# A flamingo-style gated block with routed experts: shared tiles scattered twice instead of joined by a product, and full tiles run with their gathered rows as stationary operand

## What is computed

```
# stage 1: sparse attention-like mixing of rows
sim   = mean over 4 heads of Q K^T / sqrt(32), Q = ctx Wq^T, K = ctx Wk^T
thr   = the 153rd largest value of each row of sim
A     = sigmoid(sim) where sim >= thr, else 0;  A = (A + A^T) / 2
x     = x + tanh(g_xattn) * ((1 - gamma) * layernorm(x) + gamma * A)
# stage 2: gated mixture of 8 experts, top 2 per token, plus a shared expert
n     = layernorm(x), 2048 rows
logits = n router_w; the two largest e1, e2 get the weights sigmoid(logit)
shared = silu(n sh_gate) * (n sh_up) sh_down
expert e of a token: xin = prob * n;  h = silu(xin gate_e) * (xin up_e);  y = h down_e
out   = x + tanh(g_ffn) * (shared + sum over the two experts)
```

## Time and profile before

| what | value |
|---|---|
| median of the runs | 395.9 us (395.59, 395.9, 397.62) |
| the profiled execution's own time | 397.11 us |
| its span | 395.4 us |
| TensorE busy | 367.4 us, 93% |
| VectorE busy | 256.2 us, 65% |
| ScalarE busy | 212.1 us, 54% |
| POOL busy (issue of its DMAs and small operations) | 142.1 us, 36% |
| mean granted TensorE clock | 0.978 |
| chain that ended last | TensorE 71%, ScalarE 8%, DMA 7%, DVE 7% |

### The profile page before, as it was taken

One profiled execution on the slowest core, in us unless ns is written; L12 is line 12 of the kernel. 1 busy time (PEld: TensorE's weight loads), 2 busy tenths in 40 slices (PEclk: granted clock), 3 DMA queues, 4 the chain that ended last, 5 costly groups with the idle time before them and its releaser, 6 DMA issues.

```text
span 395.4 us, 7266 instructions
## 1 busy us (share of the span) xinstructions
PE 367.4 (93%) x2372; PEld 233.0 (59%) x2374; DVE 256.2 (65%) x858; ACT 212.1 (54%) x406; POOL 142.1 (36%) x114
## 2 busy tenths in 40 slices
PE   8957889989999999999999999999999999999970
PEld 4313478557845588457875475757545644567750
DVE  1799999999999689960846793645547654623310
ACT  3595788476653686435220575554556565652320
POOL 2200220030533342222215265463656655644422
PEclk9986999999999999999999999999999999999996
DMA  7999971166657633449241755544535353644244
GB/s 218 383 388 382 389 242 37 27 195 182 189 108 170 200 64 34 72 112 206 35 53 35 128 79 90 103 77 85 87 78 91 72 86 76 107 61 87 44 55 53
DMA packets 29357, 51.18 MB, mean 129 GB/s; under 512 B 4614, under 2 KB 7942, under 8 KB 29318
## 3 DMA queue, kind: packets, MB, share of 16 engines
q0 software_dynamic: 9920, 22.16, 34.1%
q1 hardware_dynamic: 19110, 28.40, 20.8%
q10 hardware_dynamic: 288, 0.13, 0.1%
HBM read 28.60 MB, written 22.09 MB: 128 GB/s over the span
## 4 chain that ended last, share of the span: by engine, by line
PE 71%; ACT 8%; DMA 7%; DVE 7%; issue 3%; POOL 1%; SPq 1%; POOLq 1%; DVEq 0%; ACTq 0%
PE gate_up L1317 25%; PE down L1367 15%; PE gate_up L1326 8%; PE gate_up L1332 6%; PE down L1358 4%; PE turned_x L1295 4%; DMA out_dram<-y_sb,idx 3%; ACT junk L713 3%; PE front L1274 2%; DMA xs<-in_x_dram 2%; DMA out_dram<-y_sb,tmp 1%; DMA out_dram<-tmp,idx 1%; PE front L1182 1%; ACT x L750 1%; ACT sim L708 1%
## 5 line engine op out<-in xcount | busy, mean ns | idle before, releaser
L1317 PEld LDWEIGHTS gate_up<-xT,w_shgu 128*128 128x128 f32 x1024 | 117.6, 192 | 11.7 <-issue 10.4
L1317 PE MATMUL gate_up<-xT,w_shgu 128*128 128x128 f32 x1024 | 121.0, 276 | 1.5 <-ACT xT L761 1.1
L565 POOL DMA_INDIRECT xg<-x_rows,idx x34 | 52.2, 1534 | 43.5 <-DMA x_rows<-payl 13.5
L589 POOL DMA_INDIRECT out_dram<-y_sb,idx x20 | 35.9, 1793 | 54.0 <-DMA out_dram<-y_sb,idx 20.9
L815 ACT ACTIVATE y_sb<-down,gates 128x512 f32<-128x512 f32 x42 | 28.8, 687 | 36.5 <-PE down L1367 24.9
L1367 PE MATMUL down<-w_dn,hT 128*128 x100 | 47.0, 596 | 0.0
L2045 DVE COPY sim<-w_gu 128x2048 f32 x36 | 42.1, 1221 | 1.9 <-issue 1.0
L713 ACT ACTIVATE junk<-sim,probe 128x512 int8<-128x512 f32 x44 | 31.2, 712 | 16.8 <-DVE probe L1730 9.9
L2053 DVE COPY w_shgu<-w_gu 128x2048 f32 x16 | 20.0, 1249 | 26.6 <-PE gate_up L1317 17.7
L826 ACT COPY xs<-w_dn 128x1024 f32 x36 | 36.0, 1045 | 2.0 <-issue 1.7
L2074 DVE SCALAR_TENSOR_TENSOR h<-gate_up,p_t,silu 128x256 f32<-128x256 f32 x18 | 8.7, 482 | 42.9 <-ACT silu L784 33.9
(11 more groups left out here) (241 smaller groups left out, 535.0 us busy)
## 6 DMA issues: line engine op xcount, KB each, us to landing
w_gu<-in_L_ffn_gate_up_w_dram SPq DMA_DIRECT2D x8, 1024.0 KB
xs<-in_x_dram SPq DMA_DIRECT2D x4, 1024.0 KB, 7.7
w_dn<-in_L_ffn_down_w_dram SPq DMA_DIRECT2D x8, 512.0 KB
out_dram<-xs SPq DMA_DIRECT2D x4, 1024.0 KB, 6.0
x_rows<-x SPq DMA_DIRECT2D x4, 1024.0 KB, 4.7
out_dram<-y_sb POOLq DMA_DIRECT2D x16, 256.0 KB
w_gu<-in_ctx_dram SPq DMA_DIRECT2D x4, 256.0 KB, 5.8
xg<-x_rows,idx POOLq DMA_INDIRECT x34
```

Source lines behind the costliest of these rows:

```text
L565: G.indirect_dma_start(out=xg[:, t % XG, :], out_offset=None, in_=x2_rows[0:2 * N, :] if t < EARLY else x2_rows[:, :], in_offset=bass.Indi ...
L589: G.indirect_dma_start(out=out[0:2 * N, :] if t < EARLY else out[:, :], out_offset=bass.IndirectOffsetOnAxis(ap=rows, axis=0), in_=y_at(j) ...
L1317: mm = TE.matmul(g_b[j % 2][:, f * P:(f + 1) * P], w_shgu[:, c, f * P:(f + 1) * P], xT[:, x_slot(j), c], start=(c == 0), stop=(c == DC - 1))
```

## The change

- `fold`, `folded_y` and `fold_m` are gone. `find_twins` makes only the marks, and `scatter_rows` makes a second index column `idx_d`: the token's row for the second row of a pair, the spare row for all others. A new POOL helper `scatter_doubles(t)` sends the same output buffer a second time with `idx_d`, for the nine mixed tiles. It is placed behind `scatter(t + 1)` and waits for `scatter(t)` to have landed. The next mixed tile's scatter, the scatter of tile 32 and `y_of` of the buffer's next user wait for it.
- `STAGED`, `stage_full`, the weighing of rows (L2065) and `full_staged` are gone. All 16 full tiles from 10 on stream their weights, and all are turned by `turn_h`.
- The mixed tiles are 9, 11, 13, 15, 18, 21, 24, 27, 30 instead of 9, 12, 15, 18, 20, 22, 24, 26, 28, and the staging copies are moved with them.
- The joining product of tiles 32 and 33 stays.

```diff
-    MIXED = (9, 12, 15, 18, 20, 22, 24, 26, 28)
+    MIXED = (9, 11, 13, 15, 18, 21, 24, 27, 30)
...
             def scatter(t):
...
                 if t == PAIR:
                     rows = idx_p
+                    pool.wait_ge(doubles_out, 16 * MIX)
                     pool.wait_ge(scatter_ready, 1)
                 if m is not None:
-                    pool.wait_ge(folded, m + 1)
+                    if m:
+                        pool.wait_ge(doubles_out, 16 * m)
                     pool.wait_ge(scatter_ready, 1)
...
+            def scatter_doubles(t):
+                m = MIXED.index(t)
+                pool.wait_ge(scattered, 16 * CHAIN.index(t) + 16)
+                G.indirect_dma_start(out=out[:, :], out_offset=bass.IndirectOffsetOnAxis(ap=idx_d[:, m:m + 1], axis=0),
+                                     in_=y_at(job_of("M", t)), in_offset=None, compute_op=ALU.add
+                                     ).then_inc(doubles_out, 16)
...
             def y_of(j):
...
                 if k is not None and is_m(k):
                     act.wait_ge(scattered, 16 * CHAIN.index(JOBS[k][1]) + 16)
+                    if mixed_at(k) is not None:
+                        act.wait_ge(doubles_out, 16 * mixed_at(k) + 16)
...
-            def folded_y(j):
-                act.wait_ge(fold_ps, mixed_at(j) + 1)
-                A.copy(y_at(j), f_b[0][:, :]).then_inc(folded, 1)
...
-            def fold(j):
...
-                TE.matmul(f_b[0][:, :], fold_m[:, m * P:(m + 1) * P], y_at(j), start=True,
-                          stop=True).then_inc(fold_ps, 1)
...
-                if kind == "S" or staged(j):
+                if kind == "S":
                     for f in range(F2 // P):
...
             def find_twins(k):
...
-                    V.tensor_scalar(fold_m[:, m * P:(m + 1) * P], others, row_f[:, m:m + 1], None, ALU.is_equal)
                     ins = V.scalar_tensor_tensor(tmp_flat[:, m * P:(m + 1) * P], others, row_f[:, m:m + 1], upper[:, :],
                                                  ALU.is_equal, ALU.mult, accum_out=twin[:, m:m + 1])
...
                 V.tensor_tensor(idx_s, row_f, unused[:, 0:MIX], ALU.subtract)
+                V.tensor_scalar(idx_d, unused[:, 0:MIX], dump, None, ALU.add)
...
-            def stage_full(t):
...
-                V.tensor_copy(w_shgu[:, :, :].rearrange("p c f -> p (c f)"),
-                              w_gu[:, bass.ds(e * (DC * F2), DC * F2)]).then_inc(full_staged, 1)
...
-                if t in STAGED:
-                    dve.wait_ge(p_ready, t + 1)
-                    V.tensor_scalar(xg[:, r, 0:D], xg[:, r, 0:D], p_t[:, r:r + 1], None, ALU.mult).then_inc(rows_weighed, 1)
```

More of the change, by code:

```diff
@@ L95, in is_m, with m_count @@
         return JOBS[j][0] == "M"
-    STAGED = [t for t in range(EARLY + 1, MT) if t not in MIXED]
-    def staged(j):
-        return JOBS[j][0] == "M" and JOBS[j][1] in STAGED
-    def turned(j):
-        return is_m(j) and not staged(j)
-    def turned_count(j):
-        return sum(1 for k in range(j) if turned(k))
+    def m_count(j):
+        return sum(1 for kind, _ in JOBS[:j] if kind == "M")
     def x_slot(j):
@@ L1020, in _ @@
             y_of(26)
+            turned_h(27)
             stage_down(1, 2)
@@ L1029, in _ @@
             y_of(28)
-            stage_down(2, 0)
-            stage_down(2, 1)
-            folded_y(28)
+            turned_h(29)
+            stage_down(2, 2)
+            stage_down(2, 3)
             silu_of(30)
@@ L1035, in _ @@
             y_of(29)
-            stage_down(2, 2)
-            stage_down(2, 3)
+            turned_h(30)
+            stage_down(3, 0)
+            stage_down(3, 1)
             silu_of(31)
@@ L1044, in _ @@
             y_of(31)
-            stage_down(3, 0)
-            stage_down(3, 1)
-            folded_y(31)
+            turned_h(32)
+            stage_down(4, 0)
+            stage_down(4, 1)
             silu_of(33)
@@ L1050, in _ @@
             y_of(32)
-            stage_down(3, 2)
-            stage_down(3, 3)
+            turned_h(33)
+            stage_down(4, 2)
+            stage_down(4, 3)
             silu_of(34)
@@ L1059, in _ @@
             y_of(34)
-            stage_down(4, 0)
-            stage_down(4, 1)
-            folded_y(34)
+            turned_h(35)
+            stage_down(5, 0)
+            stage_down(5, 1)
             silu_of(36)
@@ L1083, in _ @@
             y_of(38)
-            stage_down(6, 0)
-            stage_down(6, 1)
-            folded_y(38)
+            turned_h(39)
+            stage_down(6, 2)
+            stage_down(6, 3)
             silu_of(40)
@@ L1119, in _ @@
             y_of(44)
-            folded_y(44)
+            turned_h(45)
+            stage_down(8, 2)
+            stage_down(8, 3)
             silu_of(46)
@@ L1123, in _ @@
             y_of(45)
+            turned_h(46)
             silu_of(47)
@@ L1126, in _ @@
             y_of(46)
+            turned_h(47)
             silu_of(48)
@@ L1129, in _ @@
             y_of(47)
+            turned_h(48)
             silu_of(49)
             y_of(48)
+            turned_h(49)
             y_of(49)
@@ L1321, in up @@
                     for c in range(DC):
-                        if c == DC // 2 and folds is not None:
-                            fold(folds)
                         for r in range(4):
@@ L2317, in _ @@
             stage_up(4, 3)
-            gate(35)
-            stage_full(21)
-            weight_of(21)
-            gate(36)
-            weight_of(22)
+            weight_of(17)
+            gate(32)
+            weight_of(18)
+            gate(33)
+            weight_of(19)
+            gate(34)
             stage_up(5, 0)
@@ L2326, in _ @@
             stage_up(5, 3)
+            weight_of(20)
+            gate(35)
+            weight_of(21)
+            gate(36)
+            weight_of(22)
             gate(37)
-            stage_full(23)
-            weight_of(23)
-            gate(38)
-            weight_of(24)
             stage_up(6, 0)
@@ L2335, in _ @@
             stage_up(6, 3)
+            weight_of(23)
+            gate(38)
+            weight_of(24)
             gate(39)
-            stage_full(25)
             weight_of(25)
             gate(40)
-            weight_of(26)
             stage_up(7, 0)
@@ L2344, in _ @@
             stage_up(7, 3)
+            weight_of(26)
             gate(41)
-            stage_full(27)
             weight_of(27)
@@ L2349, in _ @@
             weight_of(28)
+            gate(43)
             stage_up(8, 0)
@@ L2353, in _ @@
             stage_up(8, 3)
-            gate(43)
-            stage_full(29)
             weight_of(29)
```

166 lines of the change are left out of this document (77 added, 89 removed).

## The result

The changed kernel takes 400.4 us (median of six runs, 399.25 to 401.96), the kernel before beside it 395.9. The ratio is 1.010, with a 95% interval of 1.007 to 1.013: **slower by 1.0%**. The profiled execution took 400.57 us with a span of 398.8, against 397.11 and 395.4. The head of its page: engines' busy time with their shares, and the granted clock in 40 slices.

What follows compares the result with a forecast made beforehand. TensorE and the chain of scatters were taken as limits, with the chain deciding. TensorE would end 1.3 us earlier, the chain gain 1.5 (disturbed) to 3.7 (free); taking 1.5 from the median 395.9 gave 394.4 us, range 390.5 to 402.

Steps and rivals of the forecast that it cites:

- POOL becomes the bound: Rival: three issues on POOL between a mixed tile's scatter and the next take triples over 18.0 us; 400.7 us, chance 0.28.
- TensorE, 7.3 us less and 6 given back: On TensorE: folds, ups and weight copies save, turning costs, 7.3 us less; stalls return 3, 0.9 and 2.1; ends 1.3 earlier.
- the stall at job 27: Near 248 us, tile 11's y waits for tile 9's second scatter to free their shared buffer; TensorE stalls 3 us.
- the wait at the end: The last down waits for its turned h, which stands behind the y of job 48 on ScalarE: 2.1 us more.
- The 0.9 us for the gate: The gate of job 26 stands behind four staging copies ending near 234.5 us: 0.9 us given back on TensorE.
- The chain decides: The chain of scatters, at 5.6 us a cycle and 7.6 where doubles are awaited, sets the end rather than TensorE.
- The alternating stretch, tiles 8 to 15: Tile 10's scatter stays at 244.51; each later pair takes 5.6 + 7.6 us, 13.2 on the chain against TensorE's 12.1.
- The triples, 17.9 us: From tile 15, three tiles with one second scatter take 16.8 us plus about 1.1 for lengthened issues, level with TensorE's 18.0.
- the 18.5 that I had named as a sign of being wrong: Sign against the forecast: groups of three tiles with one second scatter taking over 18.5 us.
- Doubles land 3.5 us after their issue: A second scatter's data lands 3.5 us after its issue, bounds 3.3 and 5.5; 6.9 after the preceding scatter's start.
- The tail, 9.5 us: Tile 31's scatter goes at 375.5, tile 32 waits 7.6 us for doubles, tile 33 follows 1.85 behind, at 385.0.
- Issues held for a whole run of copies: Rival: POOL issues wait for all four staging copies, 2.3 us per mixed tile instead of 1.1; 405 us, chance 0.05.

Runs made afterwards that it cites:

- experiment 10: The changed kernel with its gate_up staging copies on VectorE cut to 64 of 2048 columns (mixed tiles use wrong weights): 392.11 us, ratio 0.9904.
- experiment 2: The changed kernel with sixteen filler products on TensorE ahead of the down of job 28: 400.42 us, ratio 1.0109.
- experiments 3 and 7: The changed kernel without its nine second scatters and their waits, 388.19 us; the changed kernel with a bounds check skipping the second scatters' spare rows, 392.59 us.
- experiment 1: The changed kernel with three output buffers from job 24 instead of 26, so job 27 shares none with tile 9: 398.33 us, ratio 1.0044.
- experiment 5: The changed kernel with each of the 36 staging copies of 2048 columns cut into four of 512: 403.56 us, ratio 1.0162.
- experiment 11: The kernel before with its gate_up staging copies cut to 64 of 2048 columns, whole-expert copies kept (mixed tiles use wrong weights): 396.52 us, ratio 1.0004.
- experiment 4: The kernel before with all full tiles streaming their weights and turned, folds and positions of mixed tiles kept: 397.23 us, ratio 1.0019.

## Why the prediction was wrong

I forecast 394.4 us, faster; it is 400.4, slower. My wide range held it, and the rival "POOL becomes the bound" had its time, 400.7. By the steps of the prediction:

- **TensorE, 7.3 us less and 6 given back:** right in its parts. Folds are gone; an up of a full tile adds 3.44 to the chain of waits in experiment 10 and shows as 3.60 in the timeline, where I took 3.49; the stall at job 27 is 3.51 (I took 3), the wait at the end 1.72 (2.1). The 0.9 us for the gate hardly came: the four copies ended at 233.22, where I had 234.5, and the turning of that h starts 0.15 us behind the down, at 233.75. The low clock I missed, 3.1 us; experiment 2 shows that its removal alone doesn't move the time by more than about 1 us.
- **The chain decides:** right for the last 55 us and for most of the loss; experiments 3 and 7 shorten it and move the time by 12.2 and 7.8 us. But from 254 to 343 us the path of the changed kernel is TensorE's, which the second scatter of tile 9 had set back, and by experiment 1 that is worth 2.1 us.
- **The alternating stretch, tiles 8 to 15: the step that failed.** I wrote that the scatter of tile 10 "stays" at 244.5 and took 7.6 + 5.6 us for a pair, with no lengthened issue in it. Reckoned from the scatter of tile 7, which came 1.0 us earlier, tile 10 was 2.0 us late: the issues of tiles 8 and 9 (2.60 and 2.49 us) fell on copies. 11 to 13 took 14.32 us (1.1 over), 13 to 15 took 13.95 (0.75 over). That is 3.9 of the 5.4 us by which the last scatter missed its 385.0 - 1.0. In experiment 10 the same stretches took 16.95 us from 7 to 10, as before (17.01), and 13.17 and 13.11: without the copies the sum comes out.
- **The triples, 17.9 us:** measured 18.16, 18.29, 18.97, 19.85 and 16.89 (from 282.19 to 374.35), mean 18.4. Without copies they take 17.2. My charge of 1.1 us for lengthened issues had the right size (1.2), but in the sum I let TensorE's 18.0 cover it, and 18.4 is over that. Two of the five are over the 18.5 that I had named as a sign of being wrong. From tile 15 to 31 it took 97.6 us instead of 96.3.
- **Doubles land 3.5 us after their issue:** 3.9 for tile 9 (5.45 from 247.40, less 1.56) and 3.7 for tile 30. I had said that two tenths more would turn the gain into nothing; my own 4 x 0.2 is 0.8 of the 1.5 us, so that sentence was wrong by half.
- **The tail, 9.5 us:** 9.68.

What I misjudged lies deeper than one size. I treated lengthened issues as a matter of POOL's room, three issues against one cycle. That bound was met only twice (at 294.45 and 312.49, where a scatter follows with 0.30 us). Mostly the long issue was the scatter's own, behind a mixed tile, and there it isn't filling room but standing on the chain: each tenth in it delays the landing, the second scatter, and the next mixed tile. A mean over all scatters, hid that the collision is tied to the order, the copies and the scatter both hanging on TensorE's slots. So the rival had the right place and nearly the right sum, with its price per issue (2.2) too high for gathers (1.1) and right or low for the scatters that matter (2.5 to 3.1). That it came within 0.3 us of the measured time is partly luck: the 2.0 us lost before tile 10 aren't in it.

Issues held for a whole run of copies, to which I gave 0.05, don't occur in this kernel, but four do with short copies (experiment 5).

Two things make the loss together, and taking either away turns it into a gain: without the copies 392.1 us, without the empty rows 392.6, each with the other still there. No run takes away both.

## What to carry to other kernels

When a change puts a step into a serial chain of transfers, price the whole cycle (issue, landing, hand-over), and give each issue the length it has beside what will run there, by place and not as a mean: what costs nothing in one order (experiment 11) can cost 8 us in the next (experiment 10). A transfer that is needed only for a few rows should move only those: with the bounds check the same idea went from 1.0% slower to 1.2% faster, and with the waits and the buffers mended to 1.9% faster (388.2 us). And what a fix gives back to one engine isn't what it gives the kernel: 6.6 us back on TensorE were 2.1 us of time (experiment 1), since another chain covered the rest.

## What the runs showed of the hardware

- An indirect DMA's issue on POOL takes 1.58 us undisturbed and 2.2 to 3.1 beside four float32 copies of 1.2 us in a row on VectorE. With the copies cut to about 0.4 us each, three issues took 4.63 to 4.76 us and ended 1.5 us behind the last copy, while others beside such copies took 1.6 to 1.9. What decides between the two, no run here tells.
- An accumulating indirect scatter whose rows are nearly all skipped (22.19 MB moved by the queue instead of 24.52) is issued just as long (1.56 us), and what waits for it starts about 1.9 us sooner.
- After TensorE had stood still from 250.54 to 254.05 us its granted clock was 0.50 until 259.9 us, although it was busy again for all but the first of these 6.8 us (from 253.1). After the wait of 1.60 us in experiment 10 its down took 1.98 us, and the clock stayed at 1.00. Sixteen filler products kept the clock at 1.00. The Trainium skill, page "TensorE: Matmul & The Clock Gate", section "What's actually happening", gives the same two levels, the lower for an idle engine and the higher for a busy one; the rows show both levels, and the lower one here during work too.
- A gather's issue was 1.72 us on average before, 1.48 in experiment 4, 1.13 after and 1.02 in experiment 10. The undisturbed price is 1.02; I had priced it at 1.58, as a scatter.
